# Autocorrelation in another order: rows to frequencies before the projections, lags chosen in two halves

## The reference, cut to what matters

```
Q = (query @ Wq + bq);  K = (key @ Wk + bk);  V = (value @ Wv + bv)   # each [4, 512, 256], cut into heads
Qf, Kf = rfft(Q, axis=2), rfft(K, axis=2)
corr_mean = irfft(Qf * conj(Kf), n=512).mean(axis=-1)                 # [4, 16 heads, 512 lags]
w, idx = top_k(corr_mean, 6);  w = softmax(w)
out[l] = sum over the six lags of w * V[(l + idx) % 512]
x = x + out @ Wo + bo
```

## Time and profile before

| | |
|---|---|
| median of 3 runs | 2942.86 us (2933.46 to 2942.95) |
| the profiled execution, whole | 2929.17 us |
| its span, first to last instruction | 2927.3 us |
| mean granted clock of PE | 0.945 of full speed |
| PE busy | 2737.6 us, 94% of the span |
| DVE busy | 1632.8 us, 56% |
| ACT busy | 1575.9 us, 54% |
| phase 2 on PE | 895.18 to 1093.47 us, 198.3 us |

### The profile page before, as it was taken

The page is one execution under the profiler, slowest core; times in us unless marked ns, Lnnn a source line. Parts: engine busy times, 40 slices in busy tenths (PEclk is TensorE's granted clock), DMA queues, the critical chain, the costliest instruction groups (busy, mean ns, idle before and its releaser), DMA issues.

```text
span 2927.3 us, 38802 instructions
## 1 busy us (share of the span) xinstructions
PE 2737.6 (94%) x14644; PEld 1388.8 (47%) x14644; DVE 1632.8 (56%) x2972; ACT 1575.9 (54%) x2681; POOL 307.1 (10%) x256
## 2 busy tenths in 40 slices
PE   7999999998899899998899999979989999999996
PEld 3434344343477766776333333257743343434333
DVE  5768777776474454442111221045667777777854
ACT  1677777777300112010677878922137777777753
POOL 2010100100110101121010010021211001010001
PEclk7899999999899999999999999989969999999978
DMA  5432343330200002000734535030042343234200
GB/s 112 68 39 31 56 50 53 46 45 2 93 1 29 1 1 65 1 1 30 119 45 68 68 59 68 9 91 1 7 61 46 46 68 37 32 57 49 32 8 22
DMA packets 69016, 125.55 MB, mean 43 GB/s; under 512 B 21008, under 2 KB 45528, under 8 KB 65376
## 3 DMA queue, kind: packets, MB, share of 16 engines
q1 hardware_dynamic: 67680, 120.64, 26.9%
q10 hardware_dynamic: 1152, 2.44, 0.3%
HBM read 42.50 MB, written 2.10 MB: 15 GB/s over the span
## 4 chain that ended last, share of the span: by engine, by line
PE 56%; DVE 4%; ACT 2%; issue 2%; SPq 2%; DMA 0%; ACTq 0%; POOL 0%; POOLq 0%; DVEq 0%
PE psum L190 35%; PE psum L708 13%; PE psum L1840 6%; DVE mpart L897 2%; ACT probs L775 2%; SPq L1013 1%; PE psum L278 1%; PE psum L1833 0%; SPq L1014 0%; PE psum L718 0%; DVE prod L1623 0%; PE psum L727 0%; DMA qst<-qp_lo 0%; DVE masked_hi L1927 0%; DVE masked_lo L1928 0%
## 5 line engine op out<-in xcount | busy, mean ns | idle before, releaser
L775 ACT ACTIVATE probs<-psum 128x512 f32<-128x512 f32 (+3 forms) x2080 | 1279.9, 693 | 390.7 <-PE psum L190 389.0
L897 DVE TENSOR_REDUCE mpart<-psum 128x2 f32<-128x804 f32 x1024 | 976.6, 991 | 316.6 <-PE psum L190 308.2
L708 PE MATMUL psum<-probs,vt 128*17 128x512 f32 (+1 forms) x4992 | 671.7, 613 | 1.2 <-ACT probs L775 1.2
L190 PE MATMUL psum<-qst,kst 50*128 50x512 f32 (+3 forms) x2496 | 611.4, 455 | 12.4 <-ACT probs L775 5.6
L190 PEld LDWEIGHTS psum<-qst,kst 50*128 50x128 f32 (+3 forms) x2496 | 271.3, 186 | 417.3 <-issue 267.4
L190 PE MATMUL psum<-kst,qst 48*128 48x402 f32 x2048 | 418.4, 430 | 46.4 <-DVE mpart L897 44.1
L190 PEld LDWEIGHTS psum<-kst,qst 48*128 48x128 f32 x2048 | 199.6, 196 | 355.5 <-issue 180.2
L190 PE MATMUL psum<-wv,ctxT 128*128 128x256 f32 (+1 forms) x624 | 181.2, 419 | 1.5 <-DVE kp_lo L878 0.5
L190 PE MATMUL psum<-ctxT,wk 128*128 128x512 f32 (+1 forms) x384 | 159.9, 547 | 23.3 <-DMA ctxT<-in_ctxT 22.3
L708 PEld LDWEIGHTS psum<-probs,vt 128*17 128x17 f32 (+1 forms) x4992 | 85.0, 96 | 199.9 <-issue 160.9
L190 PEld LDWEIGHTS psum<-wv,ctxT 128*128 128x128 f32 (+1 forms) x624 | 109.8, 194 | 78.1 <-issue 58.5
(11 more groups left out here) (308 smaller groups left out, 2727.9 us busy)
## 6 DMA issues: line engine op xcount, KB each, us to landing
kst<-kp_hi SPq DMA_DIRECT2D x144, 200.1 KB, 5.9
ctxT<-in_ctxT SPq DMA_DIRECT2D x36, 512.0 KB, 5.1
kst<-kp_lo SPq DMA_DIRECT2D x72, 200.1 KB, 5.4
qst<-qp_hi SPq DMA_DIRECT2D x144, 64.0 KB, 4.6
kst<-kp_hi SPq DMA_DIRECT2D x84, 100.1 KB, 2.9
qst<-qp_lo SPq DMA_DIRECT2D x72, 64.0 KB, 5.1
kst<-kp_lo SPq DMA_DIRECT2D x42, 100.1 KB, 2.9
stage<-in_L_ffn_W SPq DMA_DIRECT2D x16, 256.0 KB, 4.6
```

The costliest lines, as they stand in the source:

```text
L190: last = e.matmul(dst, lhsT, rhs, start=i == 0, stop=i == len(pairs) - 1)
L708: t = e.matmul(c.bank(self.acc)[32 * h:32 * h + VW, :], self.vt[0:kn, kc, self.head(g, h), :], p[0:kn, h % self.wide, :], start=kc == 0, s ...
L775: e.activation(self.probs[n % slots][0:kn, :, :], c.psum[0:kn, k:k + self.wide, :], ACT.Exp if softmax else ACT.Sigmoid, scale=DH ** -0.5) ...
L897: e.tensor_reduce(self.mpart[:, :, p * (SEQ // P) + qt, i], c.psum[:, k:k + 2, 0:MAX_WIDTH], AX.X, ALU.max).then_inc(c.drained(k), 1)
```

## The change

Phase 2 does the transform first. The rows of the normed input (`hrows`, no longer turned) and of the context (`crows`: PE turns the loaded `ctx` back into rows, step `l1_crow`, and ACT copies) go through one transform each (`l1_dft`, two steps of 8 passes of 512 columns, copied by ACT). The results, turned as the transform leaves them, are projected with Wq, Wk and Wv (`l1_spec`, two steps of 8 passes of 256 columns). The context's transform serves k and v. The bias, a constant in time, is 512 times itself at frequency zero and zero elsewhere; it is added in the copy of the first half of each spectrum, which moves to DVE. The second half stays with ACT. The normed rows are not turned any more for this phase, so for batches 0 to 2 the rows are made at the start of each batch in phase 2, not in phase 1. The choice of lags runs twice, for batches 0 and 1 and for batches 2 and 3, each in 32 partitions (`HALF`), the first of them beside the transforms of batches 2 and 3. All places in time are set anew, and the order of the biases' addition on POOL with them.

```diff
@@ FeedForward0.work (phase 1)
-                placed += spread(self.norm.steps(f + 1, g), g + 1.1, g + 1.9)
+                placed += spread(self.norm.steps(f + 1, g)[:6], g + 1.1, g + 1.9)
@@ Autocorrelation.work: places in time
-            placed += spread(self.norm.steps(f, b), b - 1, b - 0.1)
+            placed += spread(self.norm.steps(f, b)[:6], b - 1, b - 0.1)
         for b in range(BATCH):
-            placed += spread(self.linear_steps("q", b) + self.linear_steps("k", b) + self.spectrum_steps("q", b)
-                             + self.spectrum_steps("k", b) + [("l1_prod", f, b)], b, b + 1)
+            placed += spread([("l1_crow", f, b, 0), ("l1_rows", f, b), ("l1_crow", f, b, 2)], b - 0.3, b + 0.05)
+            placed += spread([("l1_dft", f, src, b, i) for src in "hc" for i in range(KC)] + self.spectrum_steps("q", b)
+                             + self.spectrum_steps("k", b) + [("l1_prod", f, b)], b + 0.05, b + 1)
...
+        for n in range(2):
+            chain = [("l1_cross", f, n), ("l1_corr", f, n)] + [("l1_term", f, n, i) for i in range(TOP)]
+            at = 2 * n + 2
...
@@ Autocorrelation.tensor
+            if kind == "l1_crow":
+                _, _, b, t0 = step
+                e.wait_ge(c.sem(f"l1_ctx_in{b}"), 16)
+                for j in range(2):
+                    for q in range(KC):
+                        at = (KC * j + q) * P
+                        t = e.transpose(bank[:, at:at + P], self.ctx[b][:, q, (t0 + j) * P:(t0 + j + 1) * P], c.ident[:, :])
+                t.then_inc(c.filled(k), 1)
+            elif kind == "l1_dft":
...
+                if src == "h":
+                    e.wait_ge(c.sem("l1_rows_made"), c.nth["l1_rows", f, b])
...
+                rows = (self.hrows if src == "h" else self.crows)[b % 2]
+                mm(e, bank, [(rows[:, q, i * P:(i + 1) * P], self.fwd[:, q, :]) for q in range(FC)]).then_inc(c.filled(k), 1)
             elif kind == "l1_spec":
...
+                    t = mm(e, bank[:, j * DM:(j + 1) * DM], [(src[:, q, at:at + P], self.w[name][:, q, :]) for q in range(KC)])
@@ Autocorrelation.vector
+            if kind == "l1_rows":
...
+                for i in range(4):
+                    t = 4 * b + i
+                    a = e.tensor_scalar(self.hrows[b % 2][:, i, :], c.x[:, t, :], c.meanvar[:, t, 0:1], c.rstd[:, t:t + 1],
+                                        ALU.subtract, ALU.mult)
+                a.then_inc(c.sem("l1_rows_made"), 1)
+            elif kind == "l1_spec" and step[4] == 0:
...
+                e.scalar_tensor_tensor(out=self.spectrum(name, b)[:, f0:f0 + 2, :], in0=self.b[name][:, :, :], scalar=float(SEQ),
+                                       in1=c.bank(k).rearrange("p (f d) -> p f d", d=DM), op0=ALU.mult,
+                                       op1=ALU.add).then_inc(c.drained(k), 1)
```

More of the change, by code:

```diff
@@ L1403, in work, with both @@
         self.cross = [c.sbuf(sc, "cross", [P, 2, NB]) for _ in range(4)]
[L1404 to L1409, removed]
+        self.hold = c.sbuf(sc, "hold", [1, NB])
+        def both(name, shape, dt=F32):
+            return [c.sbuf(sc, name, shape, dt) for _ in range(2)]
+        self.corr, self.kern = both("corr", [half, SEQ]), both("kern", [half, SEQ])
+        self.top8, self.idx, self.idxf = both("top8", [half, 8]), both("idx", [half, 8], U32), both("idxf", [half, 8])
+        self.neg, self.tot, self.wts = both("neg", [half, 1]), both("tot", [half, 1]), both("wts", [half, 8])
+        self.kernT = both("kernT", [P, FC, half])
         self.cr, self.ci, self.cr2 = (c.sbuf(sc, name, [P, 2, NB]) for name in ("cr", "ci", "cr2"))
@@ L1427, in work @@
+        for b, at in enumerate((3.3, 3.7, 4.02, 4.9)):
+            placed += spread(self.spectrum_steps("v", b), at, at + 0.2)
+        for b, at in enumerate((4.3, 5.1, 5.9, 6.5)):
+            placed += spread([("l1_out", f, b, i) for i in range(2)], at - 0.3, at - 0.02)
+            placed += spread([("l1_time", f, b, i) for i in range(KC)] + [("l1_proj", f, b, t0) for t0 in (0, 2)], at, at + 0.5)
             if b + 1 < BATCH:
-                placed += spread(self.norm.steps(f + 1, b), at + 1.2, at + 2)
+                placed += spread(self.norm.steps(f + 1, b), at + 0.6, at + 1.3)
@@ L1439, in spectrum_steps, with columns @@
         return [("l1_spec", self.f, name, b, f0) for f0 in (0, 2)]
[L1441 to L1453, removed]
+    def columns(self, n):
+        return slice(n * self.HALF, (n + 1) * self.HALF)
@@ L1472, in tensor @@
                     e.wait_ge(c.drained(k), v - 1)
[L1473 to L1476, removed]
-                else:
[L1478 to L1483, removed]
+            if kind == "l1_crow":
[7 more added lines that the diff above has]
+            elif kind == "l1_dft":
+                _, _, src, b, i = step
+                if b == i == 0 and src == "h":
+                    self.wait_weights(e)
+                if src == "h":
+                    e.wait_ge(c.sem("l1_rows_made"), c.nth["l1_rows", f, b])
+                else:
+                    for t0 in (0, 2):
+                        e.wait_ge(*self.made(("l1_crow", f, b, t0)))
+                rows = (self.hrows if src == "h" else self.crows)[b % 2]
+                mm(e, bank, [(rows[:, q, i * P:(i + 1) * P], self.fwd[:, q, :]) for q in range(FC)]).then_inc(c.filled(k), 1)
@@ L1491, in tensor @@
                 t.then_inc(c.filled(k), 1)
             elif kind == "l1_corr":
[L1493 to L1496, removed]
+                n = step[2]
+                re, im, at = self.cross[0], self.cross[2], self.columns(n)
```

207 lines of the change are left out of this document (120 added, 87 removed).

## The result

The changed kernel took 2948.15 us (median of 20 runs), the kernel before 2935.49 on the same chips (20 runs): a ratio of 1.0041, 95% interval 1.0029 to 1.0053, or about +12 us. The forecast was +14.5 us, near half a per cent. The sign and about the size are as forecast; several terms are not. (The forecast time, 2957, stood on a median of 3 runs, 2942.86; the 20 runs give 2935.49, and +14.5 on that is 2950.)

What follows compares the result with a forecast made beforehand. Phase 2 was taken as bound by PE. Work -17.8, waits net +27.4 and clock +8.5 made +18.1; phase 1's -3.6 gave +14.5 us, or 2957 on the median, with a range of 2931 to 2971.

Steps and rivals of the forecast that it cites:

- The signs named for the new profile: Phase 2 of 216 us with PE busy about 173, idle 4.9 at the start, about 8 before batch 3's first transform.
- PE's work: Phase 2: passes removed from PE against new transforms, projections, turns and second choice of lags, net -17.8 us.
- The disputed term: Second `kernT,fwd`, 32 passes of 32 columns: taken as +3.5 us, like 64 columns; by columns alone the term is -2.0.
- Waits: PE's waits in phase 2: start 4.9, rows 8.0, second `cross` 2.3, ways back 6.2, 7.1, 6.4, 3.6, last turns 1.4; 39.9 us.
- The step on batch 1: Tail of phase 2: PE has 16.4 us of steps, DVE held until 11.1 then needs 12.4; wait 7.1.
- that on the rows: Before batch 3's transform: PE wants `hrows` at 25.8, POOL's additions slow DVE until about 31.5; wait 8.0 us.
- the first way back: After the second `inv,cross`: PE needs batch 0's second half of `l1_out`, behind the search on DVE; wait 6.2 us.
- POOL's hold: POOL's additions slow DVE ahead of batch 3's `hrows`; rival without hold: wait 1.9, -7.8 on the sum, 2950 us, chance 0.1.
- The clock: Phase 2: 1.7 us of slow clock after each of six new waits, the old one gone, +8.5; ends none or +10.2.
- the rival of cold stretches that run on from wait to wait: Phase 2: prices right, but cold periods continue or POOL also holds copies reading PSUM; +8, 2965 us, chance 0.11.
- Phase 1: Six turns, 2.1 us, leave PE and 1.5 of a norm wait goes: -3.6; bounds -2.1 and -5.8.
- Faster rival: Tail of phase 2: DVE done before PE between two `l1_time`, so waits and cold stretches go; -30.1, 2927 us, chance 0.12.

Runs made afterwards that it cites:

- e1: Changed kernel with POOL's bias additions held until the first choice of lags is written; phase 2 took 208.24 us, ratio 1.0014 to the kernel before.
- e10: e9_all with batch 0's context loaded with the phase's weights and transformed ahead of batch 0's rows; phase 2 168.92 us, ratio 0.9868 to the kernel before.
- e4_turns: Changed kernel with the norm's rows and turns of batches 0 to 2 also made in phase 1, unused; phase 1 138.10 us, ratio 1.0077 to the kernel before.
- e6_outs: Changed kernel with three half steps of `l1_out` moved earlier in DVE's order; phase 2 took 200.34 us, ratio 0.9997 to the kernel before.
- e5: Changed kernel with 55 unused products on PE inside five waits, half of e3_filler's; phase 2 took 205.96 us, ratio 1.0011 to the kernel before.
- e8: Changed kernel with the choice by two batches kept, its tail in another order and other buffers; phase 2 179.99 us, ratio 0.9917 to the kernel before.
- e3_filler: Changed kernel with unused products (26, 23, 24, 24, 12) on PE ahead of five waits; phase 2 took 225.51 us, ratio 1.0083 to the kernel before.
- e9_all: e8 with all bias additions behind the first choice of lags and batch 3's norm and rows earlier on DVE; phase 2 172.34 us, ratio 0.9891.

## Why the prediction was right, step by step

The net was right (+14.5 forecast, about +12 measured, +9.1 in the two phases of the profiles), and its mechanism too: less work on PE, more than paid for by new waits on DVE's order and by the clock behind them. The signs named for the new profile came: phase 2 of 215 us (216) with 174.6 of PE busy (173). How near the net came is in part luck: in phase 2 PE's work was off by -1.0, the waits by -3.1 and the clock by +2.3, and phase 1 by -3.6.

- *PE's work, -17.8.* What is left of +16.3 after the waits and the clock below is -18.8; counted directly, 174.6 less 12.4 of slow clock against 182.6 less 1.7 gives the same. The disputed term fell as taken: 32 passes of 32 columns took 3.65, those of 64 columns 3.68. Columns don't price them.
- *Waits, 39.9 forecast, 36.9 measured* (ACT's four apart): start 4.8 (4.9), rows 7.0 (8.0), cross 2.4 (2.3), ways back 5.9, 6.0, 6.2, 3.5 (6.2, 7.1, 6.4, 3.6), last turns 1.2 (1.4). The step on batch 1 was over by 1.1, that on the rows by 1.0; all others are within 0.3. For the rows it is mostly a slip in the sum: 23.4 and 7.0 make 30.4, not 31.5, and with 30.4 the step says 6.9; the additions ended at 30.9 by the same count. For batch 1 the clock is the reason: PE needed 17.9 from the first way back, not 16.4, since its slow stretch cost 2.9, and DVE was done at 23.9 (23.5), so that part of the clock's price is hidden in a shorter wait. The 0.3 from PE's end to a copy's start is not in the rows either: `inv,freq` ended at 1051.52 and ACT began at 1051.62. Without it the first way back comes to 6.0; it measured 5.9. And for batch 2 the terms of DVE's side make 24.0, not 24.2.
- *POOL's hold* is shown by e1: 6.9 us with its slow stretch, for 7.8 in the rival. The rival fell.
- *The clock, +8.5.* Undersized. Against e10 the start loses 1.4, then 1.8, 2.9, 2.9, 2.0 and 1.6: 12.4 gross, 10.8 net of the one that is gone. I had charged each wait the 1.7 of the single case in the earlier trace rows; a fall costs 1.4 to 2.9 here, and the same wait costs differently from execution to execution: behind the last one, 3.46, the 16 passes took 8.62 in three and 10.1 in two (e4_turns, e6_outs), 1.6 and 3.1 us. The start is 7.63 + 1.94 for transform and turns, against 7.10 + 1.11 in e10. e5 shows the cause, and all four rounds of the tail paid. In between the clock came back (1.00 again by 981 to 986 us in the changed kernel), so the rival of cold stretches that run on from wait to wait fell. The Trainium skill ("TensorE: Matmul & The Clock Gate", section "HAM oscillation — how this bites in real kernels") describes a loop in which each round's wait drops the clock and each round pays again; the trace agrees with it, with 2.9, 2.9, 2.0 and 1.6 us for the four rounds of the tail.
- *Phase 1, -3.6.* The worst step: -7.2, past its bound of -5.8. That bound held the wait of 2.02 and 1.7 for its slow stretch. In the trace of before the clock fell twice: behind that wait, and once more from about 854.2, with PE busy since the first and no wait between:

```profile
846.70:850.50 3.80, 3.74 (x14) 2.86 (x14) 3.53 (x11) 0.60 (x1) 0.00 (x0) 0.60 0.00 0
...
854.00:856.00 2.00, 2.00 (x7) 1.57 (x6) 1.86 (x6) 0.00 (x0) 0.86 (x1) 0.58 0.00 0
856.00:858.00 2.00, 2.00 (x6) 1.57 (x6) 1.62 (x6) 0.23 (x1) 0.00 (x0) 0.57 0.01 4
```

  The 40 us at 0.91 above say what both cost: 0.09 x 40, or 3.6. With it, 2.1 of turns and 1.6 less waiting make 7.3 (of the 1.6 the norm's wait gave 0.5, 2.02 to 1.50, where I took 1.5; waits for `gate_v` gave 1.1). e4 gives back 6.5, with both falls and the wait of 2.03. The bound thus priced one fall where there were two, and the forecast itself none. Why the second comes is not shown.
- *Faster rival (2927).* It named its condition, DVE done before PE in the tail, and I held that DVE's prices forbade it. That was right for the order as written: each of the waits came. As a statement on the machine it was wrong: e6 took 14.8 us out with no operation faster, and e8 all of the tail's but 1.43.

So the changed kernel is slower because DVE's steps come too late for PE: the second choice of lags and `l1_out` stand where PE wants the next transform (e6 alone takes the loss away), and POOL's additions hold the rows of batch 3 (e1 alone takes most of it). The new transforms themselves pay. Not tried: the new tail in the kernel with the old transforms.

## What to carry to other kernels

When a change takes work from the engine that bounds a phase, walk through the queue of the engine that feeds it: a step placed too late there can cost more than the work saved, and its wait is paid again in clock. Price a wait on PE as its length plus 1.4 to 3.1 us of slow passes, here for waits of 3.2 us and more, and look for falls of the clock behind short ones. Before giving up on a split, order it by who waits: here the same matmuls took 215 us or 169.

## What the runs showed of the hardware beyond that

- The clock can fall with no wait before it. In e3_filler PE was busy without a break from 971.3, the product with 32 moving columns ended about 1005.6, and behind it the clock was near the 1.2 GHz level (window 1005.40 to 1009.00):

```profile
1005.40:1009.00 3.60, 3.60 (x12) 2.95 (x12) 0.74 (x5) 0.01 (x1) 0.00 (x0) 0.57 0.00 0
```

  It was so behind the same product in e4_turns and e10_ctx0, and not in the changed kernel, e1_bias or e9_all. What decides it is not shown.

- The length of a wait alone doesn't decide. Behind one of 2.39 the clock was 1.00 in the changed kernel (first row) and 0.68 in e5_filler_half (second); behind one of 2.02 it fell in phase 1 of before, behind one of 1.50 after the change it didn't. Why stays open.

```profile
1016.30:1019.80 3.50, 3.50 (x8) 0.76 (x8) 2.63 (x7) 0.00 (x0) 0.00 (x0) 1.00 0.00 0
```

```profile
1016.50:1021.70 5.20, 5.18 (x8) 1.04 (x8) 2.66 (x7) 0.00 (x0) 0.00 (x0) 0.68 0.01 3
```

- `inv,cross`, 8 passes with 32 stationary columns, takes 3.59 us, no less than 8 with 128 (3.60 for half an inverse transform in e8_tail).
